# A decoder block on one core: the state scan of a step as one instruction of 1024 elements, with the vector engine's small work ahead of it

## The reference

```
x = layernorm(x + mamba2x(x))                # two selective-scan blocks in a row
x = layernorm(x + attention(ctx, ctx, x))    # one head, 256 wide
x = layernorm(x + experts(x))                # top 2 of 8 experts, hidden width 1024
```

```
def step(h, inp):
    u_t, dt_t, B_t, C_t = inp
    dA = jnp.exp(dt_t[:, :, None] * A)
    h = h * dA + (dt_t * u_t)[:, :, None] * B_t[:, None, :]
    y = jnp.einsum('bds,bs->bd', h, C_t)
    return (h, y)
```

## Time and profile before

| | |
|---|---|
| median of 3 runs | 3762.82 us (3762.05 to 3764.14) |
| the profiled execution | 3769.06 us, its span 3767.3 us |
| mean granted PE clock | 0.872 of full speed |
| busy: DVE, PE, POOL, ACT | 3295.3, 2766.6, 2711.5, 2696.5 us |
| first product of the loop | starts at 45.6 us |
| last scan of the loop | starts at 3435.9 us |

### The profile page before, as it was taken

One profiled execution on the slowest core, in us unless ns is written; L12 is line 12 of the kernel. 1 busy time (PEld: TensorE's weight loads), 2 busy tenths in 40 slices (PEclk: granted clock), 3 DMA queues, 4 the chain that ended last, 5 costly groups with the idle time before them and its releaser, 6 DMA issues.

```text
span 3767.3 us, 51199 instructions
## 1 busy us (share of the span) xinstructions
PE 2766.6 (73%) x17178; PEld 2347.0 (62%) x17178; DVE 3295.3 (87%) x3315; ACT 2696.5 (72%) x6280; POOL 2711.5 (72%) x1335
## 2 busy tenths in 40 slices
PE   5677676766677677787777777887777687878775
PEld 3556555655556567676666666776666576767654
DVE  5999999999999999998999999998999999995100
ACT  6768686877878687877878597877868688764221
POOL 5878787878877787877778688777878787664000
PEclk7878887888888899988998799988988798999998
DMA  2231111111111224232321223223321232344664
GB/s 95 74 122 64 45 43 47 44 42 48 46 45 41 82 79 135 85 97 93 96 75 54 101 88 126 83 87 98 97 66 46 93 99 96 103 138 134 203 202 154
DMA packets 159451, 336.20 MB, mean 89 GB/s; under 512 B 27578, under 2 KB 45763, under 8 KB 158548
## 3 DMA queue, kind: packets, MB, share of 16 engines
q1 hardware_dynamic: 155234, 322.15, 26.3%
q0 software_dynamic: 3072, 8.39, 0.7%
q10 hardware_dynamic: 882, 2.38, 0.2%
HBM read 302.05 MB, written 30.80 MB: 88 GB/s over the span
## 4 chain that ended last, share of the span: by engine, by line
DVE 34%; issue 22%; POOL 16%; PE 11%; ACT 10%; DMA 6%; SPq 1%; POOLq 0%; DVEq 0%
DVE h L1073 21%; POOL hC L833 13%; DVE psX L1063 11%; ACT dA L1041 4%; PE psG L1283 3%; DMA w_down<-in_w_exp 3%; DMA w_up<-in_w_exp 2%; PE psY L1331 2%; PE psX L1315 2%; ACT xs L1016 2%; PE psG L1358 1%; PE psX L1358 1%; PE psX L1283 1%; POOL scratch L749 1%; DMA xg<-x_slots 1%
## 5 line engine op out<-in xcount | busy, mean ns | idle before, releaser
L833 POOL TENSOR_TENSOR hC<-h,cb 128x1024 f32<-128x1024 f32 x1024 | 2409.0, 2365 | 715.9 <-DVE h L1073 703.6
L1073 DVE TENSOR_TENSOR_SCAN h<-dA,psX 128x512 f32<-128x512 f32 x2048 | 2367.0, 1205 | 74.7 <-PE psX L1315 48.2
L1041 ACT ACTIVATE dA<-dt,negA 128x255 f32<-128x255 f32 x4096 | 1720.9, 500 | 338.0 <-DVE h L1073 335.1
L1331 PE MATMUL psY<-ident,hC 128*128 128x128 f32 x8192 | 1254.1, 304 | 39.8 <-DVE gT L1087 37.9
L1331 PEld LDWEIGHTS psY<-ident,hC 128*128 128x128 f32 x8192 | 1097.9, 160 | 83.4 <-DVE gT L1087 41.5
L1063 DVE TENSOR_TENSOR psX<-dtu,psX 128x1024 f32<-128x1024 f32 x692 | 836.3, 1209 | 80.2 <-PE psX L1306 41.0
L1315 PE MATMUL psX<-ident,xs 128*128 128x128 f32 x2656 | 443.0, 322 | 345.4 <-DVE h L1073 244.0
L1315 PEld LDWEIGHTS psX<-ident,xs 128*128 128x128 f32 x2656 | 362.4, 166 | 426.1 <-issue 268.7
L1016 ACT ACTIVATE xs<-dtuT,bT 128x512 f32<-128x512 f32 x664 | 441.1, 716 | 0.1
L1306 PE MATMUL psX<-bparts,sel 96*128 96x256 bf16 x692 | 209.4, 303 | 247.7 <-DVE h L1073 239.9
L1283 PE MATMUL psG<-xgT,w_up 128*128 128x128 f32 x1680 | 249.6, 296 | 68.9 <-DMA w_up<-in_w_exp 28.9
(11 more groups left out here) (203 smaller groups left out, 1972.8 us busy)
## 6 DMA issues: line engine op xcount, KB each, us to landing
cb<-c_dram SPq DMA_DIRECT2D x256, 512.0 KB, 3.8
w_up<-in_w_exp SPq DMA_DIRECT2D x268, 256.0 KB, 3.1
w_down<-in_w_exp SPq DMA_DIRECT2D x268, 256.0 KB, 3.0
xg<-x_slots SPq DMA_DIRECT2D x67, 128.0 KB, 3.0
y_slots<-yg SPq DMA_DIRECT2D x67, 128.0 KB, 2.9
x_slots<-got SPq DMA_DIRECT2D x16, 512.0 KB, 5.7
y_slots<-got SPq DMA_DIRECT2D x8, 512.0 KB, 5.7
xin<-in_xT SPq DMA_DIRECT2D x8, 256.0 KB, 4.0
```

Of the source, the lines that this page charges most:

```text
L833: eng.tensor_tensor(hC[i % NHC][:, :, :], h[i % NH][:, :, :], cw.to_broadcast([P, KI, L]), ALU.mult).then_inc(times_c, 1)
L1041: made = eng.activation(dA[j % NA][:, c, 1:L], dt[n % 2][:, c, 1:L], ACT.Exp, scale=negA[:, JOBS[n][0], c, s:s + 1])
L1073: eng.tensor_tensor_scan(h[i % NH][:, 2 * f:2 * f + 2, :].rearrange("p c t -> p (c t)"), dA[i % NA][:, 2 * f:2 * f + 2, :].rearrange("p c ...
L1331: made = eng.matmul(psY[:, tc, c * P:(c + 1) * P], hC[i % NHC][:, c, tc * P:(tc + 1) * P], ident[:, :], start=s == 0 and c == 0, stop=Fals ...
```

## The change

The two scans of a step become one of 1024 elements. The small work of a step, which stood between the two scans, stands between the product and the scan. `scanned` counts 1 for each step, and the waits on it are halved. The planner gets the constants PRODUCT = 1210 and SCAN = 2260, and its account of a step follows the new order: the waits for the decay and for POOL now come behind the small work. Since the planned times differ, pieces of all engines move to other steps.

```diff
-SUM, SPREAD, OUTER, SCALE = 1060, 280, 1060, 1340
+SUM, SPREAD, OUTER, SCALE, PRODUCT, SCAN = 1060, 280, 1060, 1340, 1210, 2260
...
             if i + 1 < STEPS:
-                begin = max(at["DVE"], fill_end[i + 1]) + (0 if is_turned(i + 1) else 1180)
-                at["DVE"] = max(begin, decay_end[i + 1], c_end.get(i + 1 - NH, never)) + 1120
+                at["DVE"] = max(at["DVE"], fill_end[i + 1]) + (0 if is_turned(i + 1) else PRODUCT)
...
-                then = at["DVE"] + 1120
+                then = at["DVE"] + SCAN
                 room = then - (OUTER if is_turned(i + 2) else SPREAD) + PE_OVER
...
             if i + 1 < STEPS:
-                at["DVE"] = scan_end[i + 1] = at["DVE"] + 1120
+                at["DVE"] = scan_end[i + 1] = max(at["DVE"], decay_end[i + 1], c_end.get(i + 1 - NH, never)) + SCAN
...
-                on.wait_ge(scanned, 2 * (i + 1))
+                on.wait_ge(scanned, i + 1)
...
-            def scan(i, f):
+            def scan(i):
...
-                eng.tensor_tensor_scan(h[i % NH][:, 2 * f:2 * f + 2, :].rearrange("p c t -> p (c t)"),
-                                       dA[i % NA][:, 2 * f:2 * f + 2, :].rearrange("p c t -> p (c t)"),
-                                       psX[i % 2][:, 2 * f:2 * f + 2, :].rearrange("p c t -> p (c t)"), 0.0,
-                                       ALU.mult, ALU.add).then_inc(scanned, 1)
+                eng.tensor_tensor_scan(h[i % NH][:, :, :].rearrange("p c t -> p (c t)"), dA[i % NA][:, :, :].rearrange("p c t -> p (c t)"),
+                                       psX[i % 2][:, :, :].rearrange("p c t -> p (c t)"), 0.0, ALU.mult, ALU.add).then_inc(scanned, 1)
...
                 if i + 1 < STEPS:
                     if not is_turned(i + 1):
                         times_wide_b(i + 1)
-                    scan(i + 1, 0)
                 if i >= 0:
                     small_work(plan.beside[i])
                 if i + 1 < STEPS:
-                    scan(i + 1, 1)
+                    scan(i + 1)
```

More of the change, by code:

```diff
@@ L770, in small_work @@
                         on.wait_ge(dt_ended, 2 * n + part + 1)
-                        on.wait_ge(scanned, 2 * S * (n - 1))
+                        on.wait_ge(scanned, S * (n - 1))
                         eng.tensor_tensor(dtu[n % 2][:, c, :], dt[n % 2][:, c, :], u[n % 2][:, c, :],
@@ L1038, in _ @@
                     on.wait_ge(dt_ended, 2 * (n + 1))
-                    on.wait_ge(scanned, 2 * (j - NA + 1))
+                    on.wait_ge(scanned, j - NA + 1)
                     for c in range(KI):
@@ L1289, in open_bank @@
                 if k[0] in "UB":
-                    on.wait_ge(scanned, 2 * STEPS)
+                    on.wait_ge(scanned, STEPS)
                 return k, bank[k]
@@ L1304, in spread_b @@
                 on.wait_ge(b_lo_done, n + 1)
-                on.wait_ge(scanned, 2 * (i - 1))
+                on.wait_ge(scanned, i - 1)
                 eng.matmul(psX[i % 2][:, KI - 1, :], sel[:, s % HALF:s % HALF + 1].to_broadcast([3 * HALF, P]), bparts[n % 2][:, s // HALF, :],
```

## The result

The changed kernel is slower: 3782.4 us (median of 5, 3775.1 to 3787.7) beside 3764.1 us (median of 5, 3762.1 to 3770.8) before; ratio 1.0046, 95% interval 1.003 to 1.0062. Forecast were 3722 us and a range of 3692 to 3757.

A forecast was written before the change was run, and what follows sets the result against it. The prediction took DVE to bound the loop, nine tenths of the span. Its terms, 46 + 9 - 4 - 7 - 3 = 41 us saved, gave a median of 3722 us, range 3692 to 3752, reaching up over rival A to 3757.

The forecast's parts named there:

- What bounds the kernel: Step loop, 3392 us: DVE is busy 3264 us (96%) and bounds it; what DVE saves in a step is the step's.
- One wide scan for two: DVE's scans in the loop: 1024 instructions go, each saving 0.045 us of overhead that shows, 46 us in all.
- Small work after the product: 92 loop steps: small work follows the product without needing it, hiding 0.10 us of dependence each, 9 us saved.
- The cover that goes: What the first scan hid in the loop: late inputs of small work, 0 us; late TensorE fills, 4 us of gain lost.
- The new table: Planner's step times: a plain step counted 0.025 us too long, so fills at 69 already late places cost 7 us.
- The tail: After the loop: four pieces of the experts' first product on TensorE move behind the loop, costing 3 us.
- Rival B: DVE's small work ahead of the scan: late inputs hold the whole scan, 52 us lost, 3774 us; chance 0.08.

The follow-up runs named there:

- small_first: The changed kernel with the small work one place earlier still, ahead of the product; a single run measured 3865.2 us.

## Why the prediction was wrong, by its own steps

- **What bounds the kernel:** right. What DVE took more or less, the loop took. But "DVE is busy" was read as "DVE works".
- **One wide scan for two, 46 us:** right. From start to start it measured 2.20 us for 2.25. The 75 ns of "Vector Engine (DVE) Microarchitecture Reference" of the Trainium skill, section 5.2, would have made it 77 us; the trace keeps to 0.045 us.
- **Small work after the product, 9 us saved:** half of it right, and this is the step that failed. The text said that small work "follows the product without needing it", and counted on "the pieces themselves and their semaphores" being the same. The distance is even shorter than I took (2516.98 to 2518.10, 1.12 us, where the scan needs 1.24), which gives 92 x 0.12 = 11 us. But the durations of the pieces were carried over from a place where POOL's `hC` had 0.2 us left to one where it has 1.4: the pieces stand until it ends, which is 64 us more in the loop.
- **The cover that goes, 0 us for late inputs:** right for what it looked at, 3.5 us measured, 2 more than before. It looked for waits, and the first half-scan covered something that is no wait: POOL's `hC`. 2.38 us of DVE's work after a scan stood against 2.37 us of POOL's, and I had both numbers, 1.24 + 1.14 in the earlier trace rows and 2365 ns on the page, and never put them side by side.
- **The new table, 4 + 7 us for late fills:** waits for fills did not grow in the changed kernel (89.2 to 88.4 us). The reason that I gave, a queue filled to the brim, was wrong, as less room showed. Without the hold they were 105.1 us on the old table and 92.5 on the new one, so the new table doesn't make fills late. By the ratios of two pairs of kernels it does cost some 10 us, near the 7 + 3 us that I had charged for fills and tail. That is luck for the 7: the profiles show longer tails (by 9.5 and 12.1 us), and no fills that came later.
- **The tail, 3 us:** right in sign; 6.6 us (330.2 to 336.8), and with the old table 327.3 us.
- **Rival B** had the right sign, place and threshold (0.45 us in each step; the hold is 64/92 = 0.70) with the wrong mechanism, late inputs, and was given 0.08. Its reason against, "1.5 us of such waits", speaks of waits and not of held instructions.

In sum, the loop: -46 - 11 + 64 - 1 + 2 = +8 us by terms (the 2 are inputs that came late), +4.6 measured. With 2.2 us in the start and 6.6 in the tail the span grew by 13.4 us; the medians differ by 18.3.

So the hold took the whole gain, and by the ratios it is the new table that puts the changed kernel clearly behind.

The trace of the kernel before had a sample. Its timelines of DVE and POOL at a place where one of POOL's own pieces ran into small work:

```profile
2842.89 0.14 DVE L1148 RECIPROCAL small<-small 128x2 f32<-128x2 f32 x1
2843.07 1.51 DVE L1151 TENSOR_SCALAR prob<-prob,small 128x256 f32<-128x256 f32 x2
```

```profile
2840.76 2.36 POOL L833 TENSOR_TENSOR hC<-h,cb 128x1024 f32<-128x1024 f32 x1
2843.08 1.08 POOL L749 TENSOR_TENSOR scratch<-scratch,gT 128x506 f32<-128x506 f32 x1
```

DVE's first L1151 starts while `hC` still runs (to 2843.12), and POOL's piece follows `hC` at once and ends at 2844.16. The view of line L1151, least, median and longest duration in ns:

```profile
L1151 DVE TENSOR_SCALAR prob<-prob,small x16: 342/350/1253, 734.0 to 3470.5; 128x256 f32<-128x256 f32 x16
```

A longest duration of 1253 beside a median of 350 was the question to ask.

## What to carry to other kernels

Before an instruction is moved, ask what the other engines do at its new place, and not only what it waits for: here a DVE instruction with two SBUF operands, or a tensor_scalar on SBUF, stood until the POOL instruction beside it had ended, and the profile booked that as busy time. Look for it in the spread of a group's durations, and keep such small work in the stretches where POOL is idle. A fusion that is good for the bulk may be undone by the few places that it shifts; fuse where nothing stands between, and leave the rest as it was.

## What the runs showed that I had not expected

- A tensor_scalar on 2 elements is held as fully as one on 256: 1703 ns in small_first in the mean, where the median before was 170.
- A mean can hide a hold. POOL's `hC` keeps a mean of 2363 to 2367 ns in all kernels in which it has its full size, and yet single ones that start behind a held form of DVE take up to 2535 ns in small_first.
- With POOL's `hC` at 730 ns, waits for TensorE's fills fall from 88.4 to 47.5 us.
- Less room for TensorE's small work does not make the fills come earlier (waits of 105.1, 107.2, 124.4 us).
